# Cross-attention and FP4 feed-forward on one core: other places of the attention's units in the four slots of a batch

## The chip, the cores and the metric

One core of one Trainium2 chip. The metric is the device time of the whole program in microseconds, the median of the runs shown. Engines: TensorE (PE in the profile, PEld its weight loads), VectorE (DVE), ScalarE (ACT), GpSimd (POOL), SyncE (SP, here only a queue that issues DMAs).

## What is computed

```python
x = x + xattn(layernorm(x), ctx)          # x: 16 x 224 x 512, ctx: 16 x 750 x 512, 16 heads of 32
#   q = ln(x) Wq + bq; k = ctx Wk + bk; v = ctx Wv + bv
#   softmax(q k^T / sqrt(32)) v, heads joined, Wo + bo
x = x + ffn(layernorm(x))                 # 512 -> 1408 (gate, up) -> 512
#   every linear of the ffn quantizes its input and its weights to FP4 (E2M1)
#   in blocks of 16 along the contraction; silu(gate) * up between them
```

## The kernel before, in words

The kernel has two parts, one behind the other: `attention` (16 batches of 224 query rows) and `feed_forward` (28 tiles of 128 rows). The change concerns the first.

**Numbers.** The projections are made of three passes (`PASSES`) of FP32R matmuls over a high and a low part of each operand. The high part is written by ScalarE, the low part is the rest, written by VectorE. So each projection (a unit of 12 matmuls on TensorE) is followed by a copy on ScalarE (`k`, `q`, `v`, `xt`) and, but for `v`, by a subtraction on VectorE (`k_lo`, `q_lo`, `xt_lo`).

**Groups.** The 16 heads of a batch are four groups of four (128 columns). A group t goes through: `k` (two halves of 376 and 374 keys), `q`; `mask_q` (four copies on ScalarE, which put each head's 32 rows of q into its own columns, L674); `max` (14 units: one matmul and one row maximum over half of the keys, L552 and L730) and `shift` (the negated maximum, turned and written into a row of the stacked q); `stack_low` and `stack` (24 DMAs on SyncE that stack the high and low parts of k and q under each other, L980, L989, L993); `score` (12 units of two matmuls, L566, each followed by an exp on ScalarE, L631); `pv` (three units, 0 to 2, of 32 matmuls on tiles of 32 columns, L581 and L587: probs times values, and probs times ones for the sums); then `inverse` (two reciprocals, L781), `heads` (L785), `heads_hi` (ScalarE), `sum_lo` (L789). Once a batch: `v` (12 units), `out` (two units of 12 matmuls of 512 columns, L542, and an addition on VectorE, L851), `load_ctx` (1.5 MB, L962), `load_x` (448 KB, L966), `norm` (statistics of x on VectorE, L796 and L799, and two steps on GpSimd), `norm2` (L846), `xt` (x turned), `ctx` (the split of the context into high and low, four copies on ScalarE, L667, and four subtractions on VectorE, L774), `load_res`, `add_bias`. Beside it a share of the feed-forward weights is quantized: `ffn_load`, nine steps `ffn_quant` on VectorE in slots 0, 1 and 3, `ffn_store`. In the last batch, where nothing of a next batch is left to prepare, slots 1 to 3 also hold the units that turn the quantized weights (`turn`, `turn_hi`, `turn_lo`) and prepare the first tiles (`first_...`).

**Order.** A batch has four slots, one for each group g. `slot_units(g, first, last)` (L172) makes the list of a slot: the 12 scores stand at places 0 to 11, and every other unit stands at a place of the table `PLACES[g]` (from L62); a stable sort by place gives the order. Work of other groups stands between the scores: `max` and `shift` of group g+1, `k`, `q`, `mask_q` of group g+2, `inverse` to `sum_lo` of group g-1, `v` of this batch (slots 0 and 1: the second half) or the next (slots 2 and 3). A `pv` place of 12 or more means the next slot, at that place less 12 (`attend_units`, L166). All engines run through the same list, each issues only its own part of each unit, in that order, and waits for semaphores in between. So a place sets the order on every engine and in SyncE's queue at once. What the places don't set: `stack_low` (0.1) and `stack` (0.12) stand at the head of the slot in which group g+1 gets its maxima, `ffn_store` at 0.2, `ffn_load` at 0.3, both loads of the next batch at 2.6 of slot 0.

**Banks and waits.** The projections share two banks of PSUM in turn (`proj_bank`), in the order in which they stand in the list; `max` and `shift` share three (`max_bank`); the scores two. A projection waits until VectorE or ScalarE has read the unit that had its bank before (`freed`). `k_lo` writes `k_low`, of which there is one for all groups, so its first half waits until `stack_low` of the group before has landed:

```python
elif kind == "k_lo":
    ...
    dve.wait_ge(hi_done["k"], count(b, *k))
    if u[2] == 0:
        reached(dve, stacked[t % 2], stack_count(b, t - 2))
        reached(dve, low_stacked, low_count(b, t - 1))
```

`stack_low` of group t waits on SyncE for `k_lo` and `q_lo` of t and for the last score of group t-2. `load_ctx` and `load_x` stand behind `stack` of slot 0 in SyncE's queue, and `stack_low` of slot 1 behind them. `norm` waits for x, `inverse` for the last `pv` of its group:

```python
elif kind == "norm":
    n = 2 * (b + t) + u[2]
    reached(dve, x_loaded, 16 * (b + t + 1))
    nc.vector.bn_stats(stats[:, u[2], :], xn[:, u[2], :]).then_inc(stats_done, 1)
```

Of the kernel before, what the change touches and what calls it, by code (L numbers as in the profile page):

```python
# [51 lines left out]
def reached(engine, sem, count):  # L52

    if not isinstance(count, int) or count > 0:
# [6 lines left out]

PLACES = (  # L62
    {
        "max": (0.33, 0.37, 0.51, 1.8, 1.99, 2.05, 4.01, 4.64, 4.69, 6.6, 6.7, 7.57, 8.2, 8.79),
        "shift": 9.92,
        "pv": (11.15, 13.92, 13.92),
        "inverse": (1.59, 2.47),
        "heads": 3.47,
        "heads_hi": 6.91,
        "sum_lo": 8.05,  # L70
        "k": (3.01, 5.26),
        "k_lo": (5.47, 7.13),
        "q": 7.96,
        "mask": (8.26, 8.96, 9.66, 10.36),
        "q_lo": 8.16,
        "v": (1.16, 9.3, 9.64),
        "out": (0.05, 10.75),
        "ctx": (0.05, 6.03, 6.92, 11.12),
        "xt": (0.05, 0.05),
        "xt_lo": (0.1, 5.76),  # L80
        "norm": (0.05, 1.32),
        "norm2": (0.65, 1.88),
        "load": 2.6,
        "load_res": 6.6,
        "add_bias": 11.9,
        "ffn_quant": (4.81, 4.84, 6.4, 6.97, 8.82, 9.44, 9.81, 10.38, 10.99),
    },
    {
        "max": (0.05, 0.05, 0.15, 0.74, 1.36, 2.86, 3.79, 3.99, 5.73, 7.15, 8.21, 8.55, 9.04, 9.28),
        "shift": 11.74,  # L90
        "pv": (11.75, 12.84, 12.84),
        "inverse": (2.39, 3.15),
        "heads": 5.32,
        "heads_hi": 5.86,
        "sum_lo": 11.9,
        "k": (0.05, 3.03),
        "k_lo": (1.34, 4.97),
        "q": 8.06,
        "mask": (8.36, 9.06, 9.76, 10.46),
        "q_lo": 8.5,  # L100
        "v": (6.67, 8.6, 10.24),
        "out": (0.38, 5.68),
        "ctx": (0.07, 0.07, 0.99, 5.0),
        "xt": (0.05, 0.98),
        "xt_lo": (4.3, 11.83),
        "norm": (1.37, 7.04),
        "norm2": (3.67, 8.36),
        "load": 2.6,
        "load_res": 6.6,
        "add_bias": 11.9,  # L110
        "ffn_quant": (0.05, 0.24, 1.91, 2.36, 2.86, 5.48, 6.63, 7.87, 8.1),
    },
    {
        "max": (0.05, 0.05, 1.01, 1.7, 2.25, 4.04, 4.69, 5.36, 6.56, 7.03, 7.68, 9.5, 9.51, 10.31),
        "shift": 11.19,
        "pv": (11.3, 11.68, 12.21),
        "inverse": (5.64, 7.58),
        "heads": 9.13,
        "heads_hi": 8.52,
        "sum_lo": 11.82,  # L120
        "k": (5.16, 7.43),
        "k_lo": (5.53, 9.19),
        "q": 8.7,
        "mask": (9.0, 9.7, 10.4, 11.1),
        "q_lo": 11.71,
        "v": (3.76, 7.05, 10.45),
        "out": (11.12, 11.66),
        "ctx": (0.05, 0.53, 0.64, 0.65),
        "xt": (1.48, 4.23),
        "xt_lo": (1.77, 4.6),  # L130
        "norm": (6.27, 11.9),
        "norm2": (0.05, 9.62),
        "load": 2.6,
        "load_res": 6.6,
        "add_bias": 11.9,
        "ffn_quant": (5.33, 7.73, 8.21, 8.66, 9.42, 9.43, 9.88, 11.15, 11.15),
    },
    {
        "max": (0.05, 0.05, 0.05, 0.32, 0.37, 0.4, 3.62, 5.56, 6.03, 6.65, 6.9, 7.08, 8.38, 8.78),
        "shift": 10.16,  # L140
        "pv": (8.66, 12.75, 12.89),
        "inverse": (0.26, 0.35),
        "heads": 0.61,
        "heads_hi": 6.62,
        "sum_lo": 9.74,
        "k": (1.19, 6.66),
        "k_lo": (1.54, 7.33),
        "q": 4.22,
        "mask": (4.52, 5.22, 5.92, 6.62),
        "q_lo": 4.26,  # L150
        "v": (2.18, 10.07, 11.51),
        "out": (0.55, 2.42),
        "ctx": (0.61, 0.61, 1.07, 3.43),
        "xt": (5.01, 5.81),
        "xt_lo": (11.02, 11.9),
        "norm": (0.05, 2.44),
        "norm2": (5.48, 10.01),
        "load": 2.6,
        "load_res": 6.6,
        "add_bias": 11.9,  # L160
        "ffn_quant": (4.06, 4.27, 4.52, 5.17, 6.95, 8.01, 8.05, 9.15, 10.46),
    },
)

# [1355 lines left out]
```

## Time and profile before

| | |
|---|---|
| median of 3 runs | 2176.15 us (2173.25 to 2178.88) |
| the profiled execution | 2174.35 us, its span 2172.5 us |
| granted TensorE clock, mean | 0.992 of full speed |
| busy, share of the span | PE 96%, PEld 83%, DVE 77%, ACT 40%, POOL 7% |
| attention, first score to the last batch's end | 50 to about 1473 us |
| a full batch without a stall | 87.0 us |
| DMA | 248.69 MB, mean 114 GB/s |

The profile page gives busy times of each engine, the span in 40 slices, the chain that ended last, the groups of instructions that cost most and the DMA issues. PE's busy time is modelled (matmuls are pipelined), so nearly full is not at its peak. The timeline of a window lists instructions in order of time, those of one line merged, with the idle time of the engine ahead of them and what ended it in brackets. Batches are counted from 0 here, slots and groups from 0 to 3.

### The profile page before, as it was taken

How to read it: one execution, taken by the hardware profiler on the slowest of the kernel's cores; microseconds unless marked ns; L12 is line 12 of the kernel's file. 1: busy time of each engine (PE TensorE's matmuls, PEld its weight loads, DVE VectorE, ACT ScalarE, POOL GpSimd, SP SyncE). 2: the span in 40 equal slices, each digit the busy share in tenths (PEclk: the TensorE clock that was granted, in tenths of full speed). 3: DMA queues.
4: the chain of work that ended last, by engine and by line, in shares of the span. 5: the costliest groups of instructions: out<-in, count | busy, mean ns of one | idle time of the engine just before them, and what ended most of it. 6: DMA issues, size and time to landing. Idle time of an engine off the chain costs nothing. (4 is left out here: it accounts for less than half of the span.)

```text
span 2172.5 us, 42294 instructions
## 1 busy us (share of the span) xinstructions
PE 2090.3 (96%) x16862; PEld 1799.9 (83%) x16862; DVE 1681.3 (77%) x2811; ACT 863.0 (40%) x1753; POOL 144.1 (7%) x162
## 2 busy tenths in 40 slices
PE   6999999999999999999999999978999999999998
PEld 5888888888888888889888888857787887887786
DVE  5677777777777776777777777867898988998985
ACT  5555455455554554545445555442111111111111
POOL 0000000000000000000000000001110001000100
PEclk9999999999999999999999999999999999999999
DMA  4443444534444445344453453443433443334331
GB/s 158 117 123 94 126 105 121 137 95 118 129 100 123 106 122 138 91 115 105 123 131 96 118 139 90 115 137 114 115 112 102 127 118 107 107 122 123 107 111 42
DMA packets 144675, 248.69 MB, mean 114 GB/s; under 512 B 31984, under 2 KB 89328, under 8 KB 142048
## 3 DMA queue, kind: packets, MB, share of 16 engines
q1 hardware_dynamic: 143760, 244.68, 41.5%
q8 instruction: 134, 2.20, 0.4%
q10 hardware_dynamic: 720, 1.31, 0.2%
q14 instruction: 61, 0.50, 0.1%
HBM read 101.23 MB, written 48.89 MB: 69 GB/s over the span
## 5 line engine op out<-in xcount | busy, mean ns | idle before, releaser
L730 DVE TENSOR_REDUCE row_max<-max_bank 128x1 f32<-128x376 f32 (+1 forms) x896 | 450.4, 537 | 162.4 <-PE max_bank L552 161.5
L631 ACT ACTIVATE probs<-score_bank 125x448 f32<-125x448 f32 x768 | 399.7, 541 | 290.5 <-PE score_bank L566 287.6
L526 PE MATMUL proj_bank<-attention_operands 128*128 128x256 f32 x2304 | 304.7, 282 | 0.0
L566 PE MATMUL score_bank<-qstack,kstack 103*128 103x224 f32 x1536 | 300.0, 282 | 1.4 <-DMA kstack<-k_low 1.3
L504 PE MATMUL proj_bank<-attention_operands 128*128 128x376 f32 (+1 forms) x1536 | 292.0, 339 | 8.3 <-DVE k_low L752 4.8
L526 PEld LDWEIGHTS proj_bank<-attention_operands 128*128 128x128 f32 x2304 | 288.9, 189 | 0.1
L566 PEld LDWEIGHTS score_bank<-qstack,kstack 103*128 103x128 f32 x1536 | 256.0, 191 | 37.0 <-issue 35.1
L504 PEld LDWEIGHTS proj_bank<-attention_operands 128*128 128x128 f32 x1536 | 264.6, 191 | 11.9 <-DVE k_low L752 6.4
L1339 ACT ACTIVATE f_act_gate<-gate_bank 128x512 f32<-128x512 f32 (+1 forms) x84 | 47.2, 562 | 554.4 <-PE up_bank L1279 554.4
L1279 PE MATMUL gate_bank<-gate_up,early 128*128 128x512 f32 (+1 forms) x1008 | 234.1, 382 | 23.9 <-DVE f_hidden L1435 22.0
L1279 PEld LDWEIGHTS gate_bank<-gate_up,early 128*128 128x128 f32 x1008 | 186.2, 191 | 63.5 <-issue 32.3
L1279 PE MATMUL up_bank<-gate_up,early 128*128 128x512 f32 (+1 forms) x1008 | 229.5, 377 | 0.0
L581 PE MATMUL pv_bank<-probs,values 125*32 125x224 f32 x3072 | 219.6, 358 | 0.0
L587 PE MATMUL pv_bank<-probs,ones 125*32 125x224 f32 x3072 | 216.4, 354 | 0.0
L1279 PEld LDWEIGHTS up_bank<-gate_up,early 128*128 128x128 f32 x1008 | 185.8, 189 | 30.5
L1308 PE MATMUL down_bank<-ffn_down_hi,f_hqt 128*128 128x512 f32 x616 | 197.8, 394 | 0.0
L781 DVE RECIPROCAL heads<-pv_bank 128x112 f32<-128x112 f32 x128 | 108.6, 850 | 49.5 <-PE pv_bank L587 49.5
L552 PE MATMUL max_bank<-early 128*128 128x376 f32 x448 | 131.9, 347 | 7.5 <-DVE row_max L730 6.8
L1308 PEld LDWEIGHTS down_bank<-ffn_down_hi,f_hqt 128*128 128x128 f32 x616 | 115.7, 188 | 27.3
L587 PEld LDWEIGHTS pv_bank<-probs,ones 125*32 125x32 f32 x3072 | 100.1, 110 | 46.0 <-issue 0.7
L581 PEld LDWEIGHTS pv_bank<-probs,values 125*32 125x32 f32 x3072 | 86.9, 110 | 54.4 <-issue 17.8
L552 PE MATMUL max_bank<-k_high,q_masked 128*128 128x376 f32 x448 | 130.9, 344 | 0.0
(135 smaller groups left out, 2678.4 us busy)
## 6 DMA issues: line engine op xcount, KB each, us to landing
kstack<-k_low SPq DMA_DIRECT2D x256, 93.8 KB, 2.4
kstack<-early SPq DMA_DIRECT2D x256, 93.8 KB, 2.2
kstack<-k_high SPq DMA_DIRECT2D x256, 93.8 KB, 2.2
strips_scratch<-f_strips SPq DMA_DIRECT2D x25, 960.0 KB, 3.7
f_turned<-strips_scratch SPq DMA_DIRECT2D x100, 240.0 KB, 4.4
ctx_raw<-in_ctx SPq DMA_DIRECT2D x15, 1500.0 KB, 7.6
qstack<-early SPq DMA_DIRECT2D x384, 28.0 KB, 1.9
qstack<-q_part SPq DMA_DIRECT2D x384, 28.0 KB, 1.8
```

The lines of the kernel that those rows point to most:

```text
L504: last = nc.tensor.matmul(out[:, 0:hi - lo], w_hi_lo[W_K][ws][:, c, g * P:(g + 1) * P], ctx_part[cs][:, c, lo:hi], start=(n == 0), stop=(n ...
L526: last = nc.tensor.matmul(out[:, 0:256], ctx_part[cs][:, c, kt * KW:kt * KW + P], w_hi_lo[W_V][ws][:, c, half * 256:(half + 1) * 256], sta ...
L552: nc.tensor.matmul(out[:, 0:hi - lo], masked_columns[t % 2][:, m * P:(m + 1) * P], k_part[t % 2][0][:, lo:hi], start=True, stop=True).then ...
L566: last = nc.tensor.matmul(score_bank[j % 2][:, k * SQ:(k + 1) * SQ], kstack[t % 2][0:STK, j, kt * KW:kt * KW + P], qstack[t % 2][:, j, :], ...
L581: last = nc.tensor.matmul(pv_bank[j * DK:(j + 1) * DK, 0:SQ], values[:, t % NG // 2, kt, col:col + DK], probs[p][:, j, k, :], start=(kt == ...
L587: last = nc.tensor.matmul(pv_bank[j * DK:(j + 1) * DK, SQ:2 * SQ], ones[0:KW, :], probs[p][:, j, k, :], start=False, stop=(kt == KT - 1), ...
L631: nc.scalar.activation(probs[p][:, j, :, :], score_bank[j % 2][0:KW, 0:2 * SQ].rearrange("p (k q) -> p k q", k=2), ACT.Exp, scale=float(DK ...
L730: nc.vector.tensor_reduce(row_max[:, m, kh:kh + 1], mbank[:, 0:KSPLIT[kh + 1] - KSPLIT[kh]], AX.X, ALU.max).then_inc(max_reduced, 1)
L781: nc.vector.reciprocal(heads[:, half], pv_bank[:, SQ + half.start:SQ + half.stop])\
L1279: last = nc.tensor.matmul(banks[par][:, 0:w], xqt[n % 2][xs_][:, kc, :], ffn[m][ws][:, kc, chunk(c)], start=(k == 0), stop=(k == 11))
L1308: last = nc.tensor.matmul(down_bank[n % 2][:, :], hqt[hs][:, m, :], ffn[2][ws][:, m, :], start=(m == 0 and k == 0), stop=(m == FC - 1 and ...
L1339: nc.scalar.activation(act_gate[par][:, 0:w], gate_bank[par][:, 0:w], ACT.Silu).then_inc(silu_done, 1)
```

## The change

Only the numbers of `PLACES` change: nearly all places in all four slots. The places of `load`, `load_res` and `add_bias` stay. Masks are on ScalarE before and after. The diff, cut to the lines spoken of:

```diff
 PLACES = (
     {
...
-        "pv": (11.15, 13.92, 13.92),
-        "inverse": (1.59, 2.47),
-        "heads": 3.47,
...
+        "pv": (8.39, 16.52, 16.52),
+        "inverse": (0.05, 3.64),
+        "heads": 6.31,
...
-        "ffn_quant": (4.81, 4.84, 6.4, 6.97, 8.82, 9.44, 9.81, 10.38, 10.99),
+        "ffn_quant": (6.2, 8.44, 9.06, 11.9, 11.9, 11.9, 11.9, 11.9, 11.9),
     },
     {
-        "max": (0.05, 0.05, 0.15, 0.74, 1.36, 2.86, 3.79, 3.99, 5.73, 7.15, 8.21, 8.55, 9.04, 9.28),
+        "max": (0.05, 0.05, 0.24, 1.04, 1.71, 2.15, 3.95, 4.3, 4.87, 6.3, 6.74, 7.29, 9.2, 9.32),
...
-        "pv": (11.75, 12.84, 12.84),
-        "inverse": (2.39, 3.15),
+        "pv": (11.65, 14.48, 14.69),
+        "inverse": (4.3, 6.69),
...
-        "k": (0.05, 3.03),
-        "k_lo": (1.34, 4.97),
+        "k": (0.05, 0.36),
+        "k_lo": (0.28, 0.45),
...
-        "out": (0.38, 5.68),
+        "out": (0.05, 2.33),
...
-        "norm": (1.37, 7.04),
-        "norm2": (3.67, 8.36),
+        "norm": (0.05, 4.27),
+        "norm2": (2.8, 11.9),
...
-        "ffn_quant": (0.05, 0.24, 1.91, 2.36, 2.86, 5.48, 6.63, 7.87, 8.1),
+        "ffn_quant": (0.14, 0.17, 0.98, 2.55, 2.84, 4.8, 5.61, 6.19, 8.03),
     },
     {
...
-        "pv": (11.3, 11.68, 12.21),
-        "inverse": (5.64, 7.58),
+        "pv": (11.94, 11.98, 12.19),
+        "inverse": (2.3, 5.5),
...
-        "ctx": (0.05, 0.53, 0.64, 0.65),
-        "xt": (1.48, 4.23),
+        "ctx": (0.05, 0.05, 0.05, 0.05),
+        "xt": (0.05, 4.23),
...
     },
     {
...
-        "pv": (8.66, 12.75, 12.89),
-        "inverse": (0.26, 0.35),
+        "pv": (11.7, 11.7, 11.7),
+        "inverse": (0.05, 1.93),
...
-        "ffn_quant": (4.06, 4.27, 4.52, 5.17, 6.95, 8.01, 8.05, 9.15, 10.46),
+        "ffn_quant": (2.94, 7.9, 8.01, 8.44, 8.85, 8.99, 10.85, 11.45, 11.45),
     },
 )
```

The head of slot 1, as the sort gives it in a full batch ([1,0,0] is the score unit of group 1, pass 0, head 0; the two digits behind a kind are group and part, -1 the batch before):

```
before: [1,0,0] max20 max21 ffn_quant k30 stack_low2 stack2 max22 ffn_store ffn_quant out-10 max23
        [1,0,1] k_lo30 max24 norm10 ffn_quant pv01 pv02 [1,0,2] ffn_quant inverse00 max25 ffn_quant
        [1,0,3] k31 ...
after:  [1,0,0] max20 max21 out-10 norm10 k30 stack_low2 stack2 ffn_quant ffn_quant ffn_store max22
        k_lo30 k31 k_lo31 ffn_quant [1,0,1] max23 max24 [1,0,2] max25 out-11 ffn_quant norm2 ...
        [1,0,3] max26 [1,1,0] norm11 max27 inverse00 pv01 pv02 ...
```

## Rows read from the trace of the kernel before

**Rows 1.** Windows by batch: us, busy PE, PEld, DVE, ACT, POOL; PEclk, DMA share, GB/s.

```profile
572.70:659.70 87.00, 87.00 (x863) 76.55 (x861) 65.05 (x136) 45.74 (x98) 4.66 (x7) 1.00 0.44 116
...
921.90:1012.60 90.70, 88.82 (x863) 78.19 (x862) 65.09 (x136) 45.74 (x98) 4.61 (x6) 0.98 0.43 112
...
1362.90:1473.20 110.30, 93.03 (x879) 74.05 (x877) 76.69 (x156) 47.08 (x98) 7.06 (x8) 0.94 0.41 119
```

**Rows 2.** Waits of PE, 136 to 1363 us (batches 1 to 14): total, times, longest.

```profile
PE proj_bank L504 <- DVE k_low L752: 4.8, 7, 1.9
```

**Rows 3.** Waits of DVE in the same stretch.

```profile
DVE k_low L752 <- DMA kstack<-k_low: 36.0, 14, 4.6
```

**Rows 4.** Timeline of PE, a lone pv in slot 3 of batch 6: start, us.

```profile
653.85 0.34 PE L552 MATMUL max_bank<-early 128*128 128x376 f32 x1
654.13 0.58 PE L581 MATMUL pv_bank<-probs,values 125*32 125x224 f32 x8
...
654.91 0.56 PE L581 MATMUL pv_bank<-probs,values 125*32 125x224 f32 x8
655.29 0.56 PE L587 MATMUL pv_bank<-probs,ones 125*32 125x224 f32 x8
655.78 0.44 PE L552 MATMUL max_bank<-early 128*128 128x374 f32 x1
```

**Rows 5.** Timeline of PE, slot 1 of batch 6, from its first score.

```profile
592.75 0.48 PE L566 MATMUL score_bank<-qstack,kstack 103*128 103x224 f32 x2
...
593.42 2.23 PE L504 MATMUL proj_bank<-attention_operands 128*128 128x376 f32 x12
595.49 0.34 PE L552 MATMUL max_bank<-early 128*128 128x376 f32 x1
595.67 0.39 PE L542 MATMUL proj_bank<-wo_hi,o_part 128*112 128x512 f32 x1
...
598.45 0.34 PE L552 MATMUL max_bank<-early 128*128 128x374 f32 x1
...
603.00 2.23 PE L504 MATMUL proj_bank<-attention_operands 128*128 128x374 f32 x12
```

**Rows 6.** Timeline of DVE, the same stretch.

```profile
594.38 0.51 DVE L1019 TENSOR_REDUCE fw_amax<-fw_share 128x22 f32<-128x352 f32 x1
...
596.33 0.17 DVE L1021 TENSOR_SCALAR fw_scale<-fw_amax 128x22 f32<-128x22 f32 x1
...
601.00 0.61 DVE L752 SCALAR_TENSOR_TENSOR k_low<-proj_bank,biases,k_high 128x376 fp32r<-128x376 f32 x1 [1.20 <-DMA kstack<-k_low]
601.52 0.54 DVE L730 TENSOR_REDUCE row_max<-max_bank 128x1 f32<-128x376 f32 x1
601.98 0.68 DVE L796 BATCH_NORM_STATS2 stats<-xn 112x6 f32<-112x512 f32 x1
...
602.80 0.26 DVE L1023 RECIPROCAL fw_inv_scale<-fw_scale 128x22 f32<-128x22 f32 x1
```

**Rows 7.** Timeline of SP's queue, batch 6, and its end in slot 3.

```profile
571.51 2.42 SPq L980 DMA_DIRECT2D kstack<-k_low  x4
...
590.52 0.43 SPq L962 DMA_DIRECT2D ctx_raw<-in_ctx  x1
591.00 0.43 SPq L966 DMA_DIRECT2D xn<-in_x  x1
591.54 2.41 SPq L980 DMA_DIRECT2D kstack<-k_low  x4
...
655.91 0.43 SPq L969 DMA_DIRECT2D res<-in_x  x1
```

**Rows 8.** The loads of the context (L962) and of x (L966), issue to landing.

```profile
DMA to landing us min/median/max: 6.5/7.6/9.3
...
DMA to landing us min/median/max: 3.8/10.1/11.1
```

**Rows 9.** Timeline of DVE, slot 1 of batch 0.

```profile
79.21 0.61 DVE L752 SCALAR_TENSOR_TENSOR k_low<-proj_bank,biases,k_high 128x376 fp32r<-128x376 f32 x1 [8.12 <-DMA kstack<-k_low]
```

More of the change, by code:

```diff
@@ L63 @@
     {
-        "max": (0.33, 0.37, 0.51, 1.8, 1.99, 2.05, 4.01, 4.64, 4.69, 6.6, 6.7, 7.57, 8.2, 8.79),
-        "shift": 9.92,
-        "pv": (11.15, 13.92, 13.92),
-        "inverse": (1.59, 2.47),
-        "heads": 3.47,
[L69 to L82, printed above, removed]
+        "max": (0.05, 0.77, 0.86, 1.62, 2.87, 3.35, 3.84, 4.11, 5.13, 6.02, 6.23, 6.57, 8.01, 9.14),
+        "shift": 10.83,
+        "pv": (8.39, 16.52, 16.52),
+        "inverse": (0.05, 3.64),
+        "heads": 6.31,
+        "heads_hi": 10.56,
+        "sum_lo": 11.9,
+        "k": (1.49, 4.44),
+        "k_lo": (3.19, 8.37),
+        "q": 6.51,
+        "mask": (8.75, 9.17, 9.28, 9.53),
+        "q_lo": 7.31,
+        "v": (3.55, 10.22, 11.9),
+        "out": (0.11, 2.92),
+        "ctx": (8.82, 9.05, 9.79, 9.96),
+        "xt": (9.91, 11.72),
+        "xt_lo": (4.51, 4.63),
+        "norm": (1.41, 11.58),
+        "norm2": (0.53, 8.85),
         "load": 2.6,
@@ L85 @@
         "add_bias": 11.9,
-        "ffn_quant": (4.81, 4.84, 6.4, 6.97, 8.82, 9.44, 9.81, 10.38, 10.99),
+        "ffn_quant": (6.2, 8.44, 9.06, 11.9, 11.9, 11.9, 11.9, 11.9, 11.9),
     },
     {
-        "max": (0.05, 0.05, 0.15, 0.74, 1.36, 2.86, 3.79, 3.99, 5.73, 7.15, 8.21, 8.55, 9.04, 9.28),
-        "shift": 11.74,
-        "pv": (11.75, 12.84, 12.84),
-        "inverse": (2.39, 3.15),
-        "heads": 5.32,
-        "heads_hi": 5.86,
-        "sum_lo": 11.9,
-        "k": (0.05, 3.03),
-        "k_lo": (1.34, 4.97),
[L98 to L101, printed above, removed]
-        "out": (0.38, 5.68),
-        "ctx": (0.07, 0.07, 0.99, 5.0),
-        "xt": (0.05, 0.98),
-        "xt_lo": (4.3, 11.83),
-        "norm": (1.37, 7.04),
-        "norm2": (3.67, 8.36),
+        "max": (0.05, 0.05, 0.24, 1.04, 1.71, 2.15, 3.95, 4.3, 4.87, 6.3, 6.74, 7.29, 9.2, 9.32),
+        "shift": 11.46,
+        "pv": (11.65, 14.48, 14.69),
+        "inverse": (4.3, 6.69),
+        "heads": 7.32,
+        "heads_hi": 10.26,
+        "sum_lo": 11.9,
+        "k": (0.05, 0.36),
+        "k_lo": (0.28, 0.45),
+        "q": 7.07,
+        "mask": (7.31, 8.06, 9.63, 10.12),
+        "q_lo": 7.14,
+        "v": (6.07, 8.67, 10.15),
+        "out": (0.05, 2.33),
+        "ctx": (0.05, 0.36, 4.56, 6.01),
+        "xt": (11.9, 11.9),
+        "xt_lo": (0.48, 6.68),
+        "norm": (0.05, 4.27),
+        "norm2": (2.8, 11.9),
         "load": 2.6,
@@ L110 @@
         "add_bias": 11.9,
-        "ffn_quant": (0.05, 0.24, 1.91, 2.36, 2.86, 5.48, 6.63, 7.87, 8.1),
+        "ffn_quant": (0.14, 0.17, 0.98, 2.55, 2.84, 4.8, 5.61, 6.19, 8.03),
     },
     {
-        "max": (0.05, 0.05, 1.01, 1.7, 2.25, 4.04, 4.69, 5.36, 6.56, 7.03, 7.68, 9.5, 9.51, 10.31),
-        "shift": 11.19,
-        "pv": (11.3, 11.68, 12.21),
-        "inverse": (5.64, 7.58),
[L118 to L127, printed above, removed]
-        "ctx": (0.05, 0.53, 0.64, 0.65),
-        "xt": (1.48, 4.23),
-        "xt_lo": (1.77, 4.6),
-        "norm": (6.27, 11.9),
-        "norm2": (0.05, 9.62),
+        "max": (0.05, 0.05, 1.33, 1.88, 2.46, 3.69, 4.97, 5.56, 6.41, 7.0, 7.25, 9.06, 9.14, 9.78),
+        "shift": 11.9,
+        "pv": (11.94, 11.98, 12.19),
+        "inverse": (2.3, 5.5),
+        "heads": 8.25,
+        "heads_hi": 9.44,
+        "sum_lo": 10.0,
+        "k": (5.12, 6.16),
+        "k_lo": (5.56, 8.81),
+        "q": 8.54,
+        "mask": (8.7, 8.91, 9.06, 10.61),
+        "q_lo": 11.9,
+        "v": (3.57, 4.28, 9.92),
+        "out": (6.8, 7.24),
+        "ctx": (0.05, 0.05, 0.05, 0.05),
+        "xt": (0.05, 4.23),
+        "xt_lo": (0.08, 4.92),
+        "norm": (1.57, 10.88),
+        "norm2": (0.05, 0.05),
         "load": 2.6,
@@ L135 @@
         "add_bias": 11.9,
-        "ffn_quant": (5.33, 7.73, 8.21, 8.66, 9.42, 9.43, 9.88, 11.15, 11.15),
+        "ffn_quant": (0.05, 0.05, 1.58, 2.12, 2.2, 3.84, 4.04, 4.05, 5.32),
     },
     {
-        "max": (0.05, 0.05, 0.05, 0.32, 0.37, 0.4, 3.62, 5.56, 6.03, 6.65, 6.9, 7.08, 8.38, 8.78),
-        "shift": 10.16,
-        "pv": (8.66, 12.75, 12.89),
-        "inverse": (0.26, 0.35),
[L143 to L157, printed above, removed]
+        "max": (0.05, 0.05, 1.31, 1.47, 1.94, 2.32, 2.74, 3.92, 4.77, 5.03, 7.42, 7.62, 8.28, 8.78),
+        "shift": 10.47,
+        "pv": (11.7, 11.7, 11.7),
+        "inverse": (0.05, 1.93),
+        "heads": 5.17,
+        "heads_hi": 11.68,
+        "sum_lo": 11.63,
+        "k": (2.21, 8.49),
+        "k_lo": (2.52, 9.17),
+        "q": 4.07,
+        "mask": (4.53, 7.97, 9.95, 10.69),
+        "q_lo": 6.04,
+        "v": (6.36, 9.91, 11.9),
+        "out": (0.05, 10.86),
+        "ctx": (7.22, 8.3, 9.22, 10.03),
+        "xt": (0.5, 4.72),
+        "xt_lo": (11.9, 11.9),
+        "norm": (8.08, 10.32),
+        "norm2": (1.77, 10.66),
         "load": 2.6,
```

## The prediction

> **What bounds the kernel now.** I read the busy time by batch first, cut at the first score matmul of each [rows 1]: in a full batch such as the seventh (batch 6) TensorE's matmuls fill all of its 87.0 us at clock 1.00, VectorE is busy for 65.1 and ScalarE for 45.7. Batch 10 takes 90.7 us with 88.8 busy, the last one 110.3 with 93.0. So the same units in another order can win only (a) stalls of TensorE, (b) what switching between kinds of matmul costs, and can lose by new stalls. The feed-forward part behind it is not touched, and I cost it at nothing.
>
> The waits of batches 1 to 14 name one stall of TensorE, a key projection L504 that waits for VectorE's `k_lo` (L752) [rows 2]. VectorE itself waits there each time, 36.0 us in 14 times, for the DMAs of `stack_low` [rows 3]. In batch 6, slot 1 starts at 592.75, its second key projection at 603.00, 10.25 later [rows 5]; `k_lo` starts at 601.00 after 1.20 us of waiting [rows 6]. SyncE's queue says why: the context of the next batch (1.5 MB, issued 590.52) and x (591.00) stand right ahead of `stack_low` (591.54) [rows 7]. Batch 6 just does without a stall (k_lo ends 1.4 us before it is needed); read the same way, batches 1, 2, 7, 9, 10, 11, 12 and 13 don't. The periods of batches 1 to 14 sum to 1226.7 us against 14 x 87.0 = 1218; of the 8.7 above it **7.9 us** stand at this place of slot 1, 3.7 of them in batch 10.
>
> **The change, part by part.** No instruction is added or removed; unit counts per slot stay, but for the `pv` units.
>
> 1. Runs of pv. pv works on 32-column tiles, and going in and out of it costs. In the run at 654.13 [rows 4]: the max ahead takes 0.28 to the next start where a plain one takes 0.18 (595.49 to 595.67 [rows 5]); the last half-step takes 0.49 instead of 0.38; and the first unit behind it is 0.1 longer in the same way (the max at 655.78). Together 0.3 us a run. Before, a group's slot 3 ends with pv(3,0) alone and pv(3,1), pv(3,2) come in the next slot 0: 8 runs a batch. After, the three stand together at the end of slot 3: 7 runs. 16 x 0.3 = **-4.8 us**. The trace agrees here with the Trainium skill, TensorEngine Tiling (Array Packing), Key Properties, that a change of tiling mode drains TensorE.
>
> 2. Slot lengths. Two pv (1.54 and 1.63) leave slot 0 and join slot 3: slot 0 goes from 20.1 to 16.8 us (which is its length in batch 0, where it has no such pair), slot 3 from 18.75 to 21.8; slots 1 and 2 keep 25.7 and 22.4. SyncE starts `stack_low` of slot 0 when the last score of slot 3 is made. That was 1.2 us before slot 0 (571.51 against 572.7 [rows 7]). Now three pv (4.8) and a v (1.43) come between, so 5.8 us before; its queue of slot 3 ends in time (before: `load_res` 655.91 [rows 7], 15.0 after slot 3 began; the score comes 15.8 after). From there to the context's load is 19.0 us of issuing (571.51 to 590.52), so it goes out at 13.2 in slot 0, **3.6 us before slot 1** instead of 2.3: 1.3 us earlier against what waits for it.
>
> 3. Slot 1, where it is decided. The new order on VectorE is max, max, out's add, **norm**, quantize steps 1 and 2, max, k_lo; before, norm stood behind k_lo. norm needs x, which is issued 0.48 behind the context and lands 10.1 us later in the median [rows 8]. TensorE needs, from the slot's start: score 0.22, two max 0.36, out 2.78, k 2.07, max 0.17, k 2.07, score, two max, score, max 0.97; at 8.64 it wants the second `out`, whose bank k_lo has to free. k_lo ends 2.6 after x has landed: 0.1 latency, norm to the next instruction 0.82 (601.98 to 602.80), steps 1 and 2 0.57 (0.51 and 0.17, less overlap), max 0.46, k_lo 0.61, 0.05 [rows 6]. In batch 6 x lands at -2.25 - 1.3 + 0.48 + 8.3 = 5.2: no stall. In batch 10 (context issued 1.5 before the slot, x 11.0 to landing) at 8.7: stall 8.7 + 2.6 - 8.64 = 2.6. The same sum for batches 1 to 14 gives 1.4, 1.1, 0, 0.3, 0, 0, 1.4, 0, 1.2, 2.6, 1.1, 1.7, 0.8, 0.1, together **12.0 us** in place of 7.9: **+4.1**. `stack_low` itself lands earlier than that in all of them, so the DMA that is waited for changes from it to x. Queued behind norm on VectorE are max and both k_lo; who waits is `out`, then the max units, which have 2.8 us of cover in `out`.
>
> That x keeps its 10.1 us although `stack_low` is now issued 1.9 us behind it, not 0.5, I take from the landings: context 7.6, x 10.1, and k_lo 12 behind the context's issue, in the order of issue and as their sizes (1500, 448, 375 KB) would have it at one rate. The Trainium skill, DMA: Bandwidth & Descriptors, Two DMAs through the same engine are not ordered, says that descriptors of one queue start in order though completion is not assured in it; the trace agrees. By that rule the sum is as above; were the transfers served side by side, x would come up to 1.4 us earlier (rival A).
>
> 4. Batch 0. There is no `out` in slot 1 and the context goes out only 0.6 us before it (slot 0 was as short already). k_lo waits 8.1 us [rows 9] for `stack_low` and TensorE loses 7.1. After, norm waits for x until 11.0 in the slot, the max behind it is done at 13.0, and TensorE wants its bank at 5.7; pv(0,1) and pv(0,2) (3.2 us), which covered some of it, now come later. 7.4 + 1.5 + 0.2 = 9.1: **+2.0**.
>
> 5. The last batch loses some 16 us to the turning of the weights (VectorE and the loads), whose places don't move. The pv's stand where VectorE has more to do (slot 2), but one pv leaves slot 3, where it filled a wait. I take 0, bounds -2 and +2.
>
> 6. Everything else, slot by slot with the steps of [rows 4 to 6]: slot 0, pv(0,0) wants `heads` at 11.24 and gets it at 11.0; slot 2, the third score wants exp at 5.24 (4.95), v wants the last context split at 5.56 (5.35); slot 3's last pv waits for nothing. Cost 0, but these margins are 0.2 us: if each fails by 0.2, 14 x 0.6 = +8. VectorE's waits for pv in slots 1, 2 and 3 (inverse is placed ahead of them) are idle time behind which the next max has two banks of slack.
>
> Sum: -4.8 + 4.1 + 2.0 + 0 = +1.3 us against the profiled execution's 2174.35, so 2175.7. The three runs' median is 1.8 above that execution, so I say **2177.5 us**.
>
> **The rivals.** *A, faster: x doesn't stand in the way.* If x lands 1.4 earlier, the stalls of slot 1 shrink from 12.0 to about 1.6, and batch 0 costs +0.6: -4.8 - 6.3 + 0.6, about -10: 2166. For it: less is in flight behind x. Against: the order of the landings.
>
> *B, slower: norm holds VectorE in every batch.* One mechanism: the wait for x replaces the wait for k_low and is on TensorE's path whenever x lands after 6.0 in slot 1. If the context is not issued those 1.3 us earlier (SyncE reaches `stack_low` only when slot 3's queue is through, at 15.4, with 0.5 to spare, and k_lo of slot 3 must be there), each batch pays 1.3 more, and the sum of stalls is near 28 where it was 7.9: -4.8 + 20 + 3.3 = +18, 2194. It decides from some 0.8 us a batch on. The thin margins of part 6 push the same way.
>
> *C, no net difference: the terms cancel*, my forecast, own range 2170 to 2183.
>
> **The numbers.** A measurement of this kernel tells a difference from about 0.3%, 6.5 us. C gets 0.50, A 0.24, B 0.26 (its wait is certain, its size not, and the margins add to it). The range holds C, reaches down to A's 2166 with the last batch's -2, and up to two thirds of B: 2164 to 2189.
>
> **What would show it.** Right: batch periods of about 86.7 us plus the stall; slot 0 near 16.8 and slot 3 near 21.8; VectorE waits at L796 for `in_x` in nearly all batches and hardly at L752; the context issued 3.6 us before slot 1; L542 (second out) or L552 waiting for VectorE. Wrong: no wait at L796 and periods of 86.7 throughout (A), 88 us and more (B), or a wait at L566, L581 or L526 that recurs in each batch (part 6).

## The result, and the profile after

The changed kernel takes **2189.41 us** in the median of 7 runs (2183.68 to 2192.73), the kernel before 2173.91 (2171.63 to 2178.88, 7 runs on the same chip): ratio 1.0066, 95% interval 1.0049 to 1.0082. It is slower, by 0.5 to 0.8%. The profiled run took 2189.41 us with a span of 2187.6, against a span of 2172.5 before: 15.1 us to find.

I cut the span at the first score matmul of each batch again. Windows of batches 0, 8, 12 and 15 (columns as in [rows 1]):

```profile
49.60:141.80 92.20, 85.03 (x839) 74.24 (x838) 61.67 (x129) 45.50 (x97) 2.44 (x5) 0.94 0.44 109
758.50:845.10 86.60, 86.60 (x862) 76.62 (x861) 64.96 (x135) 45.94 (x98) 2.86 (x6) 1.00 0.45 116
1111.80:1203.60 91.80, 88.60 (x862) 77.70 (x861) 64.85 (x135) 45.86 (x98) 3.60 (x7) 0.98 0.44 111
1379.50:1487.50 108.00, 88.92 (x815) 71.36 (x813) 77.67 (x155) 47.06 (x98) 5.10 (x7) 0.95 0.41 116
```

Batch 8 is the only full batch without a stall: 86.6 us, TensorE busy for all of it. That is 0.4 less than the 87.0 of [rows 1], so the order is the better one where nothing is late. Batch 12 took 91.8 with 88.6 busy. The balance of the 15.1 us:

| stretch | after - before, us | made of |
|---|---|---|
| up to batch 0 | -0.5 | |
| batch 0 | +6.0 | slot 1 +2.8, slot 0 +0.2, slot 3 +3.0 (the two pv that it has taken over) |
| batches 1 to 14 | +11.1 | periods without stalls -5.1; stalls of slot 1 +16.2 |
| batch 15, to its last `out` | -2.7 | slot 0 -3.3 (the pv pair), slot 1 +1.7, slot 2 -3.5, slot 3 and the end +2.4 |
| the feed-forward part | +1.2 | 700.1 before, 701.3 after |

The pv pair of batch 0 and that of batch 15 nearly cancel. The feed-forward part took 700.1 to 702.0 us in the profiles of all kernels here, whatever their order, 702.0 in one with the order before (e12), so its +1.2 is not put down to the change. What is left is slot 1: it takes 25.68 us without a stall, and in batches 1 to 14 took 26.79, 26.62, 26.76, 26.37, 29.51, 27.40, 26.69, 25.68, 27.90, 28.71, 27.20, 30.90, 26.94 and 27.03. Together that is 25.0 us over 14 x 25.68, where the kernel before had 8.8.

Waits of VectorE in 132 to 1360 us (batches 1 to 14; line, what for, total, times, longest), to be read beside [rows 3]:

```profile
DVE row_max L730 <- PE max_bank L552: 185.7, 180, 3.8
DVE stats L796 <- DMA xn<-in_x: 38.2, 14, 4.9
...
DVE k_low L752 <- DMA kstack<-k_low: 1.3, 3, 0.6
```

and those of TensorE in the same stretch (line, what for, total, times, longest), beside [rows 2]:

```profile
PE max_bank L552 <- DVE row_max L730: 14.1, 12, 3.1
PE proj_bank L542 <- DVE k_low L752: 1.0, 2, 0.7
```

The wait of `k_lo` for `stack_low` is gone and the wait of norm for x has taken its place: 38.2 us in 14 times where it was 36.0 in 14. A sum over waits looks unchanged. What changed is what stands behind it, TensorE: the L504 of [rows 2] doesn't wait any more, and a max unit does, 12 times. Batch 6 shows the chain. Timeline of VectorE, slot 1 of batch 6 (start, us; it starts at 599.30):

```profile
603.37 0.68 DVE L851 TENSOR_TENSOR res<-proj_bank,res 112x512 f32<-112x512 f32 x1
607.07 0.69 DVE L796 BATCH_NORM_STATS2 stats<-xn 112x6 f32<-112x512 f32 x1 [3.02 <-DMA xn<-in_x]
...
608.51 0.54 DVE L730 TENSOR_REDUCE row_max<-max_bank 128x1 f32<-128x376 f32 x1
608.97 1.11 DVE L752 SCALAR_TENSOR_TENSOR k_low<-proj_bank,biases,k_high 128x376 fp32r<-128x376 f32 x2
```

TensorE, the same place:

```profile
609.11 0.43 PE L552 MATMUL max_bank<-early 128*128 128x374 f32 x1 [1.14 <-DVE row_max L730]
609.62 0.48 PE L542 MATMUL proj_bank<-wo_hi,o_part 128*112 128x512 f32 x1
```

TensorE's second max unit wants a bank that the reduction behind norm frees, then the second `out` (L542) wants k_lo's. x landed 7.7 after the slot began, 2.6 more is k_lo's end, and TensorE wanted it at 8.64: a stall of 1.7, and the slot is 27.40 - 25.68 = 1.7 longer. So the working of part 3 holds; its input doesn't. SyncE's queue ahead of slot 0 and ahead of slot 1 of that batch, beside [rows 7]:

```profile
576.93 0.43 SPq L969 DMA_DIRECT2D res<-in_x  x1
577.47 2.42 SPq L980 DMA_DIRECT2D kstack<-k_low  x4
...
593.66 0.58 SPq L946 DMA_DIRECT2D ffn_quant<-fw_share  x1
597.34 0.34 SPq L941 DMA_DIRECT2D fw_share<-in_up  x1
597.72 0.43 SPq L962 DMA_DIRECT2D ctx_raw<-in_ctx  x1
598.20 0.43 SPq L966 DMA_DIRECT2D xn<-in_x  x1
598.74 2.48 SPq L980 DMA_DIRECT2D kstack<-k_low  x4
```

The context (L962) goes out 1.58 before slot 1, not 3.6, the latest of the 14 (3.2 in the mean). Between the store of the quantized share (L946) and the load of the next share into the same tile (L941) SyncE's queue stands for 3.1 us: that load has to wait until the store has landed. It is the longest such wait but one: the 14 of batches 1 to 14 sum to 24.5 us, and to 23.5 in the kernel before. Landings of L946, L962 and L966 in the whole run (min/median/max, in that order):

```profile
DMA to landing us min/median/max: 1.8/2.1/4.0
DMA to landing us min/median/max: 6.8/7.9/9.4
DMA to landing us min/median/max: 3.7/10.1/10.9
```

x takes as long as in [rows 8]. From issue to landing it is 10.0 in the mean of batches 1 to 14, and was 9.95.

### The profile page after: what moved, and what is told of

Its sections match the earlier page's. It is cut to its first block and busy times, and to the rows that moved or that the text cites. A ratio compares the mean times of both kernels' runs of the same rounds, so it can differ in the third digit from the quotient of the medians.

```text
span 2187.6 us, 42294 instructions
## 1 busy us (share of the span) xinstructions
PE 2089.9 (96%) x16862; PEld 1800.8 (82%) x16862; DVE 1682.4 (77%) x2811; ACT 864.9 (40%) x1753; POOL 134.3 (6%) x162
## 5 line engine op out<-in xcount | busy, mean ns | idle before, releaser
L526 PE MATMUL proj_bank<-attention_operands 128*128 128x256 f32 x2304 | 307.8, 283 | 0.0
L566 PE MATMUL score_bank<-qstack,kstack 103*128 103x224 f32 x1536 | 297.5, 282 | 1.7 <-DVE qstack L741 1.6
L526 PEld LDWEIGHTS proj_bank<-attention_operands 128*128 128x128 f32 x2304 | 287.5, 189 | 5.5 <-issue 5.4
L504 PE MATMUL proj_bank<-attention_operands 128*128 128x376 f32 (+1 forms) x1536 | 288.6, 337 | 3.4 <-ACT attention_operands L667 3.1
L566 PEld LDWEIGHTS score_bank<-qstack,kstack 103*128 103x128 f32 x1536 | 257.9, 191 | 31.8 <-issue 24.6
L504 PEld LDWEIGHTS proj_bank<-attention_operands 128*128 128x128 f32 x1536 | 264.6, 190 | 7.1 <-issue 3.4
L581 PE MATMUL pv_bank<-probs,values 125*32 125x224 f32 x3072 | 220.4, 359 | 0.0
L1308 PEld LDWEIGHTS down_bank<-ffn_down_hi,f_hqt 128*128 128x128 f32 x616 | 115.7, 188 | 27.3
L581 PEld LDWEIGHTS pv_bank<-probs,values 125*32 125x32 f32 x3072 | 88.8, 110 | 52.5 <-issue 14.5
```

The lines of the kernel that those rows point to most:

```text
L504: last = nc.tensor.matmul(out[:, 0:hi - lo], w_hi_lo[W_K][ws][:, c, g * P:(g + 1) * P], ctx_part[cs][:, c, lo:hi], start=(n == 0), stop=(n ...
L526: last = nc.tensor.matmul(out[:, 0:256], ctx_part[cs][:, c, kt * KW:kt * KW + P], w_hi_lo[W_V][ws][:, c, half * 256:(half + 1) * 256], sta ...
L566: last = nc.tensor.matmul(score_bank[j % 2][:, k * SQ:(k + 1) * SQ], kstack[t % 2][0:STK, j, kt * KW:kt * KW + P], qstack[t % 2][:, j, :], ...
L581: last = nc.tensor.matmul(pv_bank[j * DK:(j + 1) * DK, 0:SQ], values[:, t % NG // 2, kt, col:col + DK], probs[p][:, j, k, :], start=(kt == ...
L1308: last = nc.tensor.matmul(down_bank[n % 2][:, :], hqt[hs][:, m, :], ffn[2][ws][:, m, :], start=(m == 0 and k == 0), stop=(m == FC - 1 and ...
```

## The experiments

All ratios are against the kernel before on the same chip, in turns with it. Two theories went in. **Deadline:** the new order wants `k_lo` out of slot 1 earlier (8.6 against 10.25) than the loads ahead of it allow; the loads are issued too late. **Norm:** it is the place of norm, ahead of k_lo, that costs.

**e1_after_loads_early.** In the changed kernel, all four slots (only slot 0 has the loads):

```diff
-        "load": 2.6,
+        "load": 0.15,
```

> The changed kernel, with the loads of the next context and of x placed right behind the stacking of slot 0 (ahead of the store and load of the weight share) instead of behind them. Theory (the stalls of slot 1 come from the loads being issued late against slot 1): the loads go out 3 to 4 us earlier, the 25 us of stalls of slot 1 in batches 1 to 14 shrink to 0 to 3, batch 0, which has no store there, gains only 0.6; periods 86.6; about 2165 us, 0.989 of the changed kernel, faster than the kernel before. Rival (the new order is slower for a reason elsewhere, or the loads moved ahead hold up something else): above 2180 us.

Measured: 2168.76 us, ratio 0.997 (0.9956 to 0.9984); from 0.66% slower to 0.3% faster than the kernel before by the place of two DMAs. Slot 1 is now 25.6 to 26.9. Stalls of 4.1 us together are left, for another cause, and the time is 3 to 4 us above what was expected. SyncE's queue in the same place:

```profile
583.84 0.58 SPq L962 DMA_DIRECT2D ctx_raw<-in_ctx  x1
584.47 0.42 SPq L966 DMA_DIRECT2D xn<-in_x  x1
584.94 0.46 SPq L946 DMA_DIRECT2D ffn_quant<-fw_share  x1
594.38 0.35 SPq L941 DMA_DIRECT2D fw_share<-in_up  x1
594.84 2.42 SPq L980 DMA_DIRECT2D kstack<-k_low  x4
```

The store stands behind 1.5 MB of context and 448 KB of x, so SyncE waits 9 us for its landing (7 to 9 in the 14 batches), and `stack_low` of slot 1 goes out 11.0 behind the context (9.0 to 11.0). So 0.15 is too early: the loads belong behind the store and ahead of the wait.

**e2_after_norm_behind.** The changed kernel, slot 1:

```diff
-        "norm": (0.05, 4.27),
+        "norm": (0.46, 4.27),
```

> The changed kernel, with the first norm of slot 1 behind both k_lo instead of ahead of the quantize steps and of the max. Theory (VectorE's wait for x is the stall): k_lo starts near 6.3 us into slot 1, stalls go, 20 us less: about 2168 us. Rival (the landing of stack_low stands right behind that of x, and k_lo is needed 1.6 us earlier than it was, so it would stall without norm too): k_lo starts 11.5 to 12.5 us behind the context's issue as in the kernel before, near 8.7 in slot 1; 0 to 5 us less: 2184 to 2189 us, and VectorE waits at L752 for stack_low.

Measured: 2185.72 us, ratio 1.0049 (1.0037 to 1.0062), only 3.7 us less than the changed kernel, and the two intervals overlap. In the profiled runs the stalls of slot 1 sum to 19.5 us, where they were 25.0. Waits of VectorE and of TensorE in 132 to 1355 us:

```profile
DVE k_low L752 <- DMA kstack<-k_low: 35.1, 13, 6.0
```

```profile
PE proj_bank L542 <- DVE k_low L752: 13.8, 10, 4.2
```

The wait has only changed its name back. In 12 of the 14 batches k_lo starts 7.4 to 9.9 after the slot's beginning, since `stack_low` lands right behind x. **The norm theory falls:** taking away the DMA that the profile names shows the next one. The longest of these stalls came in batch 12, whose slot 1 took 31.64.

**e3_before_pv_grouped.** The kernel before, slot 3: part 2's advance of SyncE's queue, with slot 1 as it was.

```diff
-        "pv": (8.66, 12.75, 12.89),
+        "pv": (11.7, 11.7, 11.7),
```

> The kernel before, with the three pv units of group 3 together at the end of slot 3 and nothing else changed. Theory: 16 runs of pv fewer at 0.3 us, 4.8 us less; slot 0 is 16.8 us long, slot 3 21.8, the loads go out 0.5 to 1.3 us earlier against slot 1 and most of the 8.8 us of stalls of its slot 1 go: together 10 to 13 us less, about 2162 us. Rival (the switching costs nothing that order can win, as its time is hidden): 2172 to 2176 us.

Measured: 2184.11 us, ratio 1.0041 (1.0028 to 1.0053). A miss on the time, but slot 1 did what the deadline theory says: 25.70 in every one of batches 1 to 14, no stall, with the context 3.2 to 4.4 ahead. Slot 0 is 16.80. Slot 3, though, takes 22.91 and not 21.8, in every batch. TensorE in slot 3 of batch 6:

```profile
657.53 0.63 PE L552 MATMUL max_bank<-early 128*128 128x376 f32 x2
658.61 0.92 PE L566 MATMUL score_bank<-qstack,kstack 103*128 103x224 f32 x4 [0.45 <-ACT probs L631]
```

In the kernel before, pv(3,0) stood at this place ([rows 4]). Without its 1.54 us the score comes before ScalarE has freed a bank, and the period is 87.88 where it was 86.99. The wait named is 0.45 us in each batch (6.3 in 14 times); what else makes the slot 1.1 longer than expected was not traced. So the pv's can't be moved by themselves; the new slot 3 spreads its scores otherwise and has no such wait.

**e4_before_loads_early.** The kernel before with `"load": 0.15`.

> The kernel before with only the loads moved as in the first kernel of this call. Theory: its stalls of slot 1 (8.8 us in batches 1 to 14) go, batch 0 gains 0.6 to 1: 2164 to 2166 us, periods 87.0. Rival: no gain, 2172 us and more, since stack_low of slot 1 is issued when the last score of slot 0 is made, and lands late for another reason.

Measured: 2169.98 us, ratio 0.9976 (0.9966 to 0.9987). The kernel before gains too, and less than the changed one does (0.24% against 0.96%). The gain is half of what was expected. As in e1, `stack_low` goes out 9 to 11 behind the context, and six batches stall for 1.3 to 2 us, 9.7 together, no less than the 8.8 before; the profiled run (2177.07) is the slowest of the ten, so where the 0.24% of the median comes from isn't shown.

**e5_after_loads_before_share** and **e6_before_loads_before_share.** `"load": 0.25` in the changed kernel and in the one before: behind the store, ahead of the share's load.

> The changed kernel with both loads of the next batch between the store and the load of the weight share in slot 0 (place 0.25). In the run with 0.15 SyncE issued stack_low of slot 1 only 9 to 11 us behind the context, as the load of the share waits for the landing of the store, which then queued behind the context. Theory: here the store goes first and lands in 2 us, the loads no longer wait for it, x and stack_low land 2.5 to 4 us earlier than in the changed kernel, k_lo of slot 1 starts before 8.0 in all batches and the 25 us of stalls of batches 1 to 14 are gone: periods 86.6, 2163 to 2166 us. Rival (the share's load then queues behind the context and holds SyncE and stack_low as in the 0.15 run): 2168 us.

> The kernel before with the loads at the same place 0.25. Theory: no stall of slot 1 in batches 1 to 14, periods 87.0, 2165 to 2167 us. The difference to the changed kernel with the same loads is then the one run of pv a batch (0.35 us x 14 = 5 us for the changed order) less what the changed order loses in batch 0 (2.9 us) and in the last batch: 0 to 2 us in its favour.

Measured: e5 2169.65 us, ratio 0.9964 (0.9949 to 0.998), span 2164.3; e6 2171.98 us, ratio 0.9974 (0.9962 to 0.9986), span 2168.0. Both medians are some 5 us above what was expected, on a chip where the kernel before took 2177.05. SyncE's queue in e5:

```profile
584.18 0.58 SPq L946 DMA_DIRECT2D ffn_quant<-fw_share  x1
584.81 0.42 SPq L962 DMA_DIRECT2D ctx_raw<-in_ctx  x1
585.28 1.83 SPq L966 DMA_DIRECT2D xn<-in_x  x1
588.10 0.33 SPq L941 DMA_DIRECT2D fw_share<-in_up  x1
588.83 2.41 SPq L980 DMA_DIRECT2D kstack<-k_low  x4
```

The store lands in 2.1 us in most batches and in 3.9 here, and most of that time goes into issuing the two loads: what SyncE still waits for it is 8.7 us in 14 times, where it was 24.5, and that lies under the context's transfer. The context is 4.4 to 5.9 ahead of slot 1, and VectorE's waits in 132 to 1355 us have shrunk from 38.2 to 8.1 between the two DMAs:

```profile
DVE k_low L752 <- DMA kstack<-k_low: 4.4, 8, 1.0
...
DVE stats L796 <- DMA xn<-in_x: 3.7, 7, 1.4
```

Ten of the 14 batches now take exactly 86.57 us, and the stalls of the other four sum to 1.5 us. The window of batch 6:

```profile
573.20:659.80 86.60, 86.60 (x862) 76.66 (x862) 65.11 (x135) 45.92 (x98) 3.68 (x7) 1.00 0.46 118
```

In e6 eight batches take 86.99, and the stalls of the rest sum to 3.4. With the loads early in both, the new order is 0.4 us a batch shorter, though the two medians don't tell the kernels apart; without, it is the slower one. Batch 0 remains: 90.04 us in e5, 85.94 in e6.

**e7_after_both.** e5, and norm behind k_lo as in e2.

> The changed kernel with the loads at 0.25 and norm behind both k_lo. Theory (x was one of two landings that stand close together, and both are early now): within 1.5 us of the same kernel with norm ahead, in batches 1 to 14 no stall in either. Rival (norm ahead of k_lo costs TensorE even without a wait, 0.8 us on VectorE in each batch): 5 us less than with norm ahead.

Measured: 2172.71 us, ratio 0.998 (0.9964 to 0.9996); the span is 2164.4, e5's, and so are the slots where nothing is late. Single late landings cost 4.3 us in its slot 1, where e5 had 1.5, and the intervals of e5 and e7 overlap. Once the loads are early, norm behind k_lo gains nothing.

**e8_after_slot1_of_before.** The changed kernel with all places of slot 1 as in the kernel before (some 20 lines), the loads at 2.6, and in slot 0 (whose last two pv places put a group's pv into slot 1):

```diff
-        "pv": (8.39, 16.52, 16.52),
+        "pv": (8.39, 13.92, 13.92),
...
-        "k": (0.05, 0.36),
-        "k_lo": (0.28, 0.45),
+        "k": (0.05, 3.03),
+        "k_lo": (1.34, 4.97),
...
-        "norm": (0.05, 4.27),
+        "norm": (1.37, 7.04),
```

> The changed kernel with the whole of slot 1 in the places of the kernel before (pv(0,1), pv(0,2) with it), slots 0, 2 and 3 as changed, loads at 2.6. Theory (the loss is slot 1's: k_lo has to be done at 8.6 us instead of 10.25 while x and stack_low land at 8 to 10): the stalls of slot 1 fall from 25 to 0 to 5 us, since the loads go out 0.8 us earlier against it than in the kernel before, with the gain of a pv run kept: 2165 to 2170 us. Rival (slots 0, 2 and 3 make the loss): above 2180 us.

Measured: 2173.32 us, ratio 0.9978 (0.9966 to 0.9989). Waits of VectorE and of TensorE in 132 to 1355 us:

```profile
DVE k_low L752 <- DMA kstack<-k_low: 27.5, 13, 4.9
```

```profile
PE proj_bank L504 <- DVE k_low L752: 3.0, 3, 2.2
```

The rival (a loss in slots 0, 2 or 3) asked for more than 2180 us. This is the run that separates lateness from deadline. The context goes out 3.0 ahead of slot 1 in the mean (changed kernel: 3.2), and k_lo starts 7.0 to 11.9 after the slot began, 8.9 in the mean (changed kernel: 7.9 to 11.6, 9.5). x and `stack_low` land 7.3 and 8.8 after the slot began, where they did at 7.5 and 9.1. The data are hardly less late, but slot 1 loses 5.7 us over its 25.59 (4.1 of them in batch 12) in place of 25.0 over 25.68: this order can do without k_lo for 1.6 us longer.

**e9_after_first_loads_at_start.** e5, with batch 0's loads of the next context and x taken out of slot 0 into the start:

```diff
-    if g == 0 and not last:
+    if g == 0 and not last and not first:
...
+    units += [("load_ctx", 1), ("load_x", 1)]
```

> The changed kernel with the loads at 0.25, and those of batch 0 (context and x of batch 1) issued at the start, behind the stacking of q of group 0, instead of in slot 0. In the 0.25 run slot 1 of batch 0 takes 28.9 us; without its two out units (5.6 us) it would take 20.1. Theory (that loss is the same late landing): slot 1 of batch 0 takes 20.1 to 21 us, 8 us less than the 0.25 run: about 2161 us, 0.9925 of the kernel before. Rival (x or k_lo is late there for another reason, or the loads disturb the start): a gain under 3 us.

Measured: **2158.9 us** (2156.27 to 2161.49), ratio **0.9925** (0.9913 to 0.9938), span 2154.5. It beats both kernels. Slot 1 of batch 0 takes 21.3 us, where it took 28.9 in e5. In batch 0 of the changed kernel TensorE's timeline had this:

```profile
79.09 0.68 PE L552 MATMUL max_bank<-early 128*128 128x374 f32 x1 [6.54 <-DVE row_max L730]
```

and in e9, whose lines stand one further down:

```profile
72.43 0.34 PE L553 MATMUL max_bank<-early 128*128 128x374 f32 x1
72.90 0.48 PE L567 MATMUL score_bank<-qstack,kstack 103*128 103x224 f32 x2
73.80 0.44 PE L553 MATMUL max_bank<-early 128*128 128x376 f32 x1 [0.42 <-DVE row_max L731]
```

Of the 6.54 and the half us behind it, 0.42 is left.

**e10_after_pv_split.** e5, in slot 3 a value projection between pv(3,0) and pv(3,1): one run of pv more a batch, the same units.

```diff
-        "pv": (11.7, 11.7, 11.7),
+        "pv": (11.7, 11.95, 11.95),
```

> The changed kernel with the loads at 0.25 and the three pv of group 3 split once more: pv(3,0), then the last v, then pv(3,1) and pv(3,2), so 8 runs of pv a batch as in the kernel before. Theory (0.3 us for each run): slot 3 takes 22.05 instead of 21.75 us in every batch, periods 86.9, 4.5 us more than the 0.25 run. Rival (the 0.35 us between 86.99 and 86.57 come from something else in the order): slot 3 stays at 21.75.

Measured: 2172.88 us (11 runs), ratio 0.9994 (0.9984 to 1.0003), where e5 has 0.9964. The window of its batch 6:

```profile
577.90:664.80 86.90, 86.90 (x864) 76.61 (x860) 64.95 (x135) 46.03 (x98) 4.38 (x7) 1.00 0.45 116
```

Slot 3 is 21.99 instead of 21.75, slot 0 16.87 instead of 16.76, the others are the same: 86.91 against 86.57, **0.34 us for a run of pv**. Over the 14 batches that is 4.8 us. The rest of the 6.5 that the ratios differ by stands in single late landings (batch 10 alone has 3.6 in its slot 1), which fall otherwise in each kernel.

**e11_after_slot1_of_before_loads** and **e12_before_first_loads_at_start.** e8 with `"load": 0.25` and e9's start; the kernel before with the same two edits.

> The changed kernel with slot 1 of the kernel before, loads at 0.25 and those of batch 0 at the start. Theory: here k_lo may be 1.6 us later than in the changed slot 1, so no batch stalls: periods 86.67 throughout, within 2 us of the changed slot 1 with the same loads, about 2161 us. A rival that the changed slot 1 is worse even when nothing is late would give 5 us less than it.

> The kernel before with loads at 0.25 and those of batch 0 at the start. Theory: slot 1 of batch 0 takes 20 to 21 us instead of 27.7, periods 87.0: about 2164 us, 3 us (one pv run a batch, 0.35 us x 14 = 5, less 2 for the last batch) more than the changed kernel with the same loads.

Measured: e11 2159.46 us, ratio 0.9923 (0.991 to 0.9935); e12 2161.79 us, ratio 0.9939 (0.9925 to 0.9953). With all loads early, slot 1 may be the old or the new one, it makes no difference that can be measured (e9, e11), and the order before comes out 0.14% behind. In e11 no batch stalls. The intervals of e9 and e12 overlap; that the new order is the shorter rests on the batch periods (86.57 and 86.99), not on these two medians. Most of the gain over the kernel before is the loads': 0.61% of e9's 0.75% comes with the order before too.

## Where the prediction was right and where it was wrong, point by point

I forecast no net difference, 2177.5 us; it came out 0.66% slower, 2189.41, 12 us above the forecast and at the very end of the range (2189). The case that came true is rival B, in a milder form than its 2194. The mechanism was right. The step that failed is **the term of part 3, the size of slot 1's stalls**: "12.0 in place of 7.9" was 25.0 in place of 8.8. Two things went into it wrongly: the issue of the context in part 2 (and with it the landing of x), and a clock taken as full behind every stall.

**Part 1, runs of pv, and part 2, slot lengths: right.** Slot 0 is 16.76 (16.8 said), slot 3 21.75 (21.8 said), and the two together are 38.51 against 38.83: 0.32 a batch, where I had 0.3. e10 puts the same run back and pays 0.34. The Trainium skill, TensorEngine Tiling (Array Packing), Key Properties, says that changing the tiling mode drains TensorE; the runs agree, at 0.3 us for a run of pv.

**Part 2, the context's issue: the step that carried most of the error.** I said 3.7 ahead in the mean of the batches (2.4 before, plus 1.3) and it is 3.2. 0.5 x 14 is **7 us**. It has two halves.

SyncE began slot 0's queue 5.5 before the slot instead of 5.8. That "its queue of slot 3 ends in time" was wrong: in 13 of 14 batches `stack_low` (L980) is issued 0.5 behind `load_res` (L969), as in batch 6 above, with no wait for the score between them, and in the 14th 1.3 behind. I had read `load_res` in batch 6 alone, 15.0 after slot 3 began; over the 14 batches of the kernel before it is 14.9 to 16.4, 15.5 in the mean. After the change it is 15.7, and the score was made at 15.6. In e3, whose `load_res` goes out earlier, the queue of slot 0 begins 5.95 ahead in every batch. Rival B named this margin.

From there to the context took 19.1 us, where it was 18.8: 20.1 to 20.7 in batches 5, 6, 10 and 12. I had taken the queue as issuing only; it also waits, for the store L946 to land, and had done so before the change. That explains batches 6 and 12 (landings of 3.7 and 4.0 in place of 2.1), and 1.0 us of the sum over 14. In batches 5 and 10 single issues took longer (four of L980 4.0 and 4.1 us, elsewhere 2.4); the runs don't show why.

x followed the context by 0.65 in the mean and not by 0.48 (in four batches SyncE paused between the two): **2.4 us**.

**Part 3, the mechanism: right.** VectorE waits at L796 in all of 14 batches and for `stack_low` hardly (1.3 us in three); x lands as long after its issue as before; k_lo starts 1.9 behind norm; the first to lack a bank is a max unit, then the second `out`. With the measured landings the formula (landing + 2.6 - 8.64) gives each stall within 0.05 us in ten of the 14 batches. In batches 4 and 9 k_lo had to wait for `stack_low` as well, which made it 0.3 and 0.6 more. In batch 12 x landed at 9.66, so 3.6; that slot, though, was 5.2 longer. Timeline of TensorE, batch 12:

```profile
1140.28 0.44 PE L552 MATMUL max_bank<-early 128*128 128x374 f32 x1 [3.12 <-DVE row_max L730]
...
1141.43 1.05 PE L542 MATMUL proj_bank<-wo_hi,o_part 128*112 128x512 f32 x2
1142.28 0.63 PE L542 MATMUL proj_bank<-wo_lo,o_part 128*112 128x512 f32 x1
...
1145.01 0.39 PE L542 MATMUL proj_bank<-wo_hi,o_part 128*112 128x512 f32 x1
```

A step of `out` takes 0.43 here (1141.43 to 1142.28, two of them), where it takes 0.23 again from 1144.8 on. Windows of one microsecond show the granted clock (us, PE busy, PEclk, DMA share, GB/s), two behind the wait of batch 12, two behind that of batch 5 (519.20), one at the same place of batch 10:

```profile
1140.70:1141.70 1.00, 0.93 (x4) 0.78 0.55 136
1141.70:1142.70 1.00, 1.00 (x3) 0.50 0.70 162
...
520.20:521.20 1.00, 1.00 (x4) 0.50 0.17 52
...
523.20:524.20 1.00, 1.00 (x6) 0.87 0.17 48
...
963.40:964.40 1.00, 1.00 (x6) 1.00 0.65 150
```

0.50 is the lower of the two levels, 1.2 GHz instead of 2.4. It cost 1.6 us here and 1.6 in batch 5 (its slot is 3.8 longer than without a stall, of which the formula gives 2.2): **3.2 us** that a sum at one clock doesn't have. The kernel before had shown it: batch 10 in [rows 1] is 3.7 us over 87.0 with only 1.9 idle, at clock 0.98, and its second key projection took 3.86 us instead of 2.23:

```profile
954.27 3.86 PE L504 MATMUL proj_bank<-attention_operands 128*128 128x374 f32 x12 [1.88 <-DVE k_low L752]
```

The balance of part 3: the formula gives 12.0 with the landings that I assumed (the terms as I printed them add up to 11.7, by rounding) and 20.6 with the measured ones. x landed 0.74 later than assumed, in the mean of the batches, 10.4 us in all: the 7 and the 2.4 above, and 1 for its longer transfer; 1.8 of it fell into slack that batches 3, 6 and 8 had. The clock adds 3.2, `stack_low` in batches 4 and 9 0.9, and 0.3 is rest: 25.0.

**"`stack_low` itself lands earlier than that in all of them"** was true of 11 of the 14 batches and misleading. It was earlier by so little that taking norm away gained 3.7 us of the 16 (e2). The cause is not that norm stands ahead of k_lo, but that the whole group (max, k_lo, second `out`) is wanted 1.6 us sooner than before, with both landings behind 1.5 MB of context. e8 shows that the places of slot 1 make the loss; that it is this one among them rests on the landings, which hardly moved.

**Part 4, batch 0:** slot 1 took 2.8 more and slot 0 0.2, where I had +2.0, so 1.0 short. Norm waited 6.99 us there; the mechanism was the one said.

**Part 5, the last batch:** +0.4 without the pv pair (-3.1), within the bound of 2, but made of larger terms. Its slot 1 takes 29.0 us in every kernel with the new slot 1, with a wait of 1.8 at the shift (L556) for VectorE's negated maximum (L735); in e8 and e11, which have the old slot 1, it takes 27.3. Slot 2, where the turned weights are waited for, takes 23.0 to 27.4 from one profile to the next. The feed-forward part, which I cost at nothing, is 1.2 longer in this profile; see the table.

**Part 6, the thin margins: right.** No wait recurs at L566, L581 or L526 in the full batches, and the period without a stall is 86.6. e3 shows that such margins are no matter of course: moving the pv's alone made one fail, 0.45 us of waiting in every batch.

**The rivals.** A needed x to land 1.4 us earlier: it didn't (10.0 against 9.95). B named the mechanism and the condition (the context is not issued 1.3 us earlier, because SyncE's queue of slot 3 is not through). The condition came true by half: 0.8 earlier, and B asked for a total near 28 where 25.0 came. In C the terms were to cancel; -5.1 did not cancel +16.2.

What stays open: why single issues and landings of SyncE's queue take longer in some batches, and what brings the clock down behind some stalls and not behind others. No run tried the new slot 3 with an earlier `load_res`.

## What to carry to other kernels

For each load, write down its landing and the time at which the busiest engine cannot go on without what depends on it, in every batch and not in one good one: an order that is shorter by 0.4 us a batch lost 16 us because it moved one such deadline 1.6 us ahead and left the loads where they were. Before a wait is removed by moving the instruction that waits, see what lands next behind it (here `stack_low` behind x); the remedy is at the issue of the loads. And a store whose landing the issuing queue waits for is a part of that queue's time: put large loads behind the store and ahead of the wait.

## What the runs showed of the hardware that was not expected

**The landing of a small store behind a large load.** The share's store (176 KB) lands 2.1 us after its issue in the median of the changed kernel, and up to 4.0. Issued 1.1 us behind the context and 0.5 behind x (e1) it took 7.4 to 9.4 us to land in batches 1 to 14, each time 0.4 to 0.6 after x, and SyncE waited for it that long. This is the order of issue again. The Trainium skill, DMA: Bandwidth & Descriptors, Two DMAs through the same engine are not ordered, has the descriptors start in order with no promise for their completion; e1's landings, context, x, store in each of the 14 batches, agree with the first. On the second the traces don't decide.

**The clock after a stall.** `out` ran at 1.2 GHz after the waits of 1.75 us in batch 5 and 3.12 us in batch 12, and at 2.4 GHz after that of 2.51 us in batch 10, each time at the same place in the order. So the length of the wait alone doesn't decide it, and no run here shows what does. In the kernel before it came behind the wait of 1.88 us in batch 10. Where it happened in the changed kernel, a stall cost 1.6 us more than its own length.
